# Mixture-of-experts tail of a transformer layer: 39 expert tiles of 128 rows become 25 full tiles and nine tiles of four 32-row units on column groups

## The reference, cut to what matters

```
logits = einsum('btd,ed->bte', x, router_w);  expert = argmax(softmax(logits))
h      = square(relu(einsum('btd,edh->ebth', x, expert_fc)))     # 256 -> 1024, expert_fc 8 x 256 x 1024
out    = einsum('ebth,edh->ebtd', h, expert_proj)                # 1024 -> 256
y      = layernorm(x + out of the token's own expert)
```

## Time and profile before

| | |
|---|---|
| median of 3 runs | 866.6 us (861.0 to 872.18) |
| the profiled execution | 864.4 us, of which the span from first to last instruction 862.6 us |
| mean granted TensorE clock | 0.989 |
| busy share of TensorE / VectorE / ScalarE / GpSimd | 94 / 68 / 32 / 35% |
| DMA | 110.62 MB, 128 GB/s over the span |

### The profile page before, as it was taken

The page is one execution under the profiler, slowest core; times in us unless marked ns, Lnnn a source line. Parts: engine busy times, 40 slices in busy tenths (PEclk is TensorE's granted clock), DMA queues, the critical chain, the costliest instruction groups (busy, mean ns, idle before and its releaser), DMA issues.

```text
span 862.6 us, 19421 instructions
## 1 busy us (share of the span) xinstructions
PE 810.9 (94%) x6910; PEld 653.6 (76%) x6911; DVE 584.7 (68%) x1359; ACT 273.7 (32%) x550; POOL 302.9 (35%) x425
## 2 busy tenths in 40 slices
PE   7979899999999999999999899899989999999995
PEld 3457677677677677677677677688979999999994
DVE  7988878888888888888888846844334444444442
ACT  2324223434434434434434233422112222222220
POOL 8211432414614614614614734633212222222222
PEclk9999999999999999999999999999999999999998
DMA  8899994101001001000000045836535555555540
GB/s 270 266 314 325 298 308 149 49 2 51 25 2 51 25 2 51 25 2 27 25 3 26 26 165 166 282 113 201 183 123 180 185 172 176 178 184 172 176 153 0
DMA packets 69722, 110.62 MB, mean 128 GB/s; under 512 B 5262, under 2 KB 54288, under 8 KB 69649
## 3 DMA queue, kind: packets, MB, share of 16 engines
q1 hardware_dynamic: 66240, 101.17, 37.7%
q0 software_dynamic: 3408, 8.46, 2.6%
HBM read 66.94 MB, written 43.58 MB: 128 GB/s over the span
## 4 chain that ended last, share of the span: by engine, by line
PE 87%; DVE 6%; issue 2%; ACT 2%; POOL 1%; DMA 1%; POOLq 0%; SPq 0%; DVEq 0%; ACTq 0%
PE bank L877 16%; PE bank L866 16%; PE bank L756 7%; PE bank L768 6%; PE bank L788 6%; PE bank L799 6%; PE bank L566 5%; PE bank L718 5%; PE bank L734 4%; PE bank L682 4%; PE bank L575 2%; PE bank L710 2%; PE bank L604 2%; PE bank L596 1%; DVE cc L1302 1%
## 5 line engine op out<-in xcount | busy, mean ns | idle before, releaser
L866 PEld LDWEIGHTS bank<-xsT,fc 128*128 128x128 f32 x1248 | 148.3, 195 | 5.5 <-issue 3.7
L866 PE MATMUL bank<-xsT,fc 128*128 128x128 f32 x1248 | 149.1, 279 | 3.4 <-DVE hT L1588 3.3
L1162 POOL TENSOR_TENSOR rstd<-vare,minus_half 128x1 f32<-128x1 f32 x96 | 53.9, 564 | 266.6 <-DVE vare L1427 266.3
L1048 ACT ACTIVATE relu<-bank 128x512 f32<-128x512 f32 x78 | 46.1, 597 | 205.5 <-PE bank L866 194.9
L877 PE MATMUL bank<-pj,act 128*128 x416 | 94.5, 380 | 1.3 <-issue 1.1
L1418 DVE TENSOR_TENSOR sm<-bank,upto 128x512 f32<-128x512 f32 x128 | 79.4, 684 | 19.7 <-PE bank L682 19.7
L877 PEld LDWEIGHTS bank<-pj,act 128*128 128x128 f32 x416 | 77.0, 190 | 11.6 <-issue 2.2
L1217 POOL TENSOR_TENSOR mrstd<-mvare,minus_half 128x1 f32<-128x1 f32 x39 | 22.1, 567 | 166.0 <-DVE mvare L1606 165.1
L756 PE MATMUL bank<-n1T,w1s 128*128 128x256 f32 x256 | 67.5, 386 | 2.9 <-ACT hT L1000 2.4
L1598 DVE COPY token<-xs 128x1 int32<-128x1 int32 x39 | 6.0, 154 | 93.1 <-PE bank L877 91.6
L788 PE MATMUL bank<-n1T,w1s 128*128 128x256 f32 x256 | 66.8, 383 | 1.3 <-ACT hT L1017 0.8
(11 more groups left out here) (236 smaller groups left out, 1457.5 us busy)
## 6 DMA issues: line engine op xcount, KB each, us to landing
fc<-in_fc SPq DMA_DIRECT2D x39, 1024.0 KB, 5.1
routed_rows<-empty SPq DMA_DIRECT2D x64, 520.0 KB, 9.3
pj<-in_pj SPq DMA_DIRECT2D x8, 1024.0 KB, 11.8
xs<-routed_rows SPq DMA_DIRECT2D x39, 130.0 KB, 2.0
x<-in_x SPq DMA_DIRECT2D x8, 512.0 KB, 3.8
xT<-in_xT SPq DMA_DIRECT2D x7, 512.0 KB, 5.0
w1s<-in_w SPq DMA_DIRECT2D x1, 1024.0 KB, 7.0
w2s<-in_w SPq DMA_DIRECT2D x1, 1024.0 KB, 9.0
```

Source lines behind the costliest of these rows:

```text
L866: last = nc.tensor.matmul(h_bank[n][:, chunk(f)], fc[:, s, k, chunk(4 * n + f)], xsT[:, k, :], start=(k == 0), stop=(k == KT - 1))
L1048: nc.scalar.activation(relu[:, n], src[:], ACT.Relu).then_inc(M["relu"].sem, 1)
L1162: nc.gpsimd.tensor_tensor(rstd[:, n, c], vare[:, n, c], minus_half[:], ALU.pow)\
```

## The change

Each expert now gives only whole tiles of 128 rows to the 25 **full** tiles (`FULL`), and what is left of all experts is cut into **units** of 32 rows. Four units, each of an expert of its own, make a **mixed** tile; there are nine (36 units), at the places 11, 14, 17, 20, 23, 26, 29, 31 and 33 of 34. In a mixed tile:

- the rows of each unit are loaded with a transfer of their own (four of 32 rows), and each unit's up weights with one of 1 MB, into a ring of six buffers (`up_units`, `load_unit_up`);
- `up_mixed` has the rows as the stationary side and the weights as the moving one: 16 calls with 32 stationary and 512 moving columns, the four units on four groups of 32 columns of the array. The hidden values come out not transposed, so `turn_hidden` turns them (8 transposes) and ScalarE copies them (`take_hidden`);
- `down_mixed` has 32 calls with 32 stationary and 256 moving columns on the same groups, with the down weights of each unit in `down_units`, which ScalarE and GpSimd copy there from `pj` ahead of time (`take_down`, two each).

Full tiles from 9 on share two `fc` buffers; the third is in the ring. `units_left` (`d_units`) is a new chain of 22 steps on VectorE after the finish of tile 4, which says what the units are. In VectorE's written order the square of tile 8 now stands ahead of the finish of tile 7. The loops of tiles 9 on are written out, and `down` reads its expert's number right ahead of its first matmul. Cut to its core:

```diff
-SLOTS = NT + E - 1
+FULL = -(-(TOK - E * (P - 1)) // P)                                   # 25
+MIXED = -(-((TOK - FULL * P + E * (UNIT - 1)) // UNIT) // UPT)        # 9
+MIXED_TILES = (11, 14, 17, 20, 23, 26, 29, 31, 33)
+RING = 6
+UP_BUFFER = [n % 3 if n < EARLY else (n - EARLY) % 2 for n in range(FULL)]
...
-    ("m_finish", 4, 0), ("m_square", 6, 0), ("m_finish", 5, 0), ("m_square", 7, 0), ("m_finish", 6, 0),
-    ("m_finish", 7, 0), ("m_square", 8, 0),
+    ("m_finish", 4, 0), ("d_units", 7, 0), ("m_square", 6, 0), ("m_finish", 5, 0), ("m_square", 7, 0), ("m_finish", 6, 0),
+    ("m_square", 8, 0), ("m_finish", 7, 0),
...
+            def load_unit_up(n):
+                e = of_tile(unit_expert, n, E - 1)
+                if n >= RING:
+                    M["up"].wait(sp, MIXED_TILES[(n - RING) // UPT], 2)
+                elif n == RING - 1:
+                    M["up"].wait(sp, EARLY - 1, 2)
+                sp.dma_start(up_units[n % RING][:], fc_d[bass.ds(e, 1)].rearrange("e (k p) n -> p (e k) n", p=P))\
+                    .then_inc(units_in[n // UPT % 2], 16)
...
+            load_rows(EARLY)
+            sp.wait_ge(rt, R_UNITS)
+            for n in range(RING - 1):
+                load_unit_up(n)
+            load_rows(EARLY + 1)
+            load_unit_up(RING - 1)
+            load_rows(EARLY + 2)
+            for j in range(EARLY, SLOTS):
+
+                if of_units(j):
+                    for n in range(UPT * mixed_of(j) + RING, min(UPT * mixed_of(j) + RING + UPT, UNITS)):
+                        load_unit_up(n)
+                elif next_of_buffer(full_of(j)) is not None:
+                    load_up(next_of_buffer(full_of(j)))
+                if EARLY + 3 <= j + 2 < SLOTS:
+                    load_rows(j + 2)
...
+            def up_mixed(j):
+                i = mixed_of(j)
+                M["xsT"].wait(pe, j, 1)
+                pe.wait_ge(units_in[i % 2], 16 * UPT * (i // 2 + 1))
+                for n in range(2):
+                    free_hidden(j, n)
+                    for k in range(KT):
+                        for u in range(UPT):
+                            last = nc.tensor.matmul(h_bank[n][unit(u), :], xsT[:, k, unit(u)],
+                                                    up_units[(UPT * i + u) % RING][:, k, n * 512:n * 512 + 512],
+                                                    start=(k == 0), stop=(k == KT - 1), skip_group_check=True)
+                    last.then_inc(M["up"].sem, 1)
...
+            turn_rows(EARLY)
+            for j in range(EARLY, SLOTS):
+                (up_mixed if of_units(j) else up)(j)
+                if j + 1 < SLOTS:
+                    turn_rows(j + 1)
+                if of_units(j - 1):
+                    down_mixed(j - 1, o_bank)
+                else:
+                    down(j - 1)
+                if of_units(j):
+                    turn_hidden(j)
+            down_mixed(SLOTS - 1, pm)
...
+            def take_down(i, u):
+                if i > 0:
+                    M["down"].wait(pool, MIXED_TILES[i - 1], 1)
+                own = pool.value_load(unit_expert[0:1, UPT * i + u:UPT * i + u + 1], min_val=0, max_val=E - 1)
+                nc.gpsimd.tensor_copy(down_units[u][:], pj[:, bass.ds(own, 1)].rearrange("p a f n -> p (a f) n"))\
+                    .then_inc(own_first, 1)
```

More of the change, by code:

```diff
@@ L385, in build @@
         cleared = sem("cleared")
-        experts_in = [sem(f"expert{e}_in") for e in range(E)]
+        experts_in = sem("experts_in")
+        own_first, own_last = sem("own_first"), sem("own_last")
+        units_in = [sem("up_units_in0"), sem("up_units_in1")]
         fc_in = [sem(f"fc_in{n}") for n in range(3)]
@@ L481, in of_tile, with load_up @@
                 return sp.value_load(at, min_val=0, max_val=most)
[L483 to L494, removed]
+            def load_up(n):
+                e = of_tile(expert, n, E - 1)
+                if n >= 3:
+                    M["up"].wait(sp, max(FULL_TILES[m] for m in range(n) if UP_BUFFER[m] == UP_BUFFER[n]), 2)
+                sp.dma_start(fc[:, UP_BUFFER[n]], fc_d[bass.ds(e, 1)].rearrange("e (k p) n -> p (e k) n", p=P))\
+                    .then_inc(fc_in[UP_BUFFER[n]], 16)
@@ L502, in _ @@
                 sp.wait_ge(scattered[half], 16 * NC * groups)
[L503 to L507, removed]
+            for j in range(3):
+                load_rows(j)
+                load_up(j)
             ev["wo"].wait(sp, G - 1, NC)
@@ new lines, in turn_hidden, with down @@
+            def turn_hidden(j):
+                if mixed_of(j) > 0:
+                    M["act"].wait(pe, MIXED_TILES[mixed_of(j) - 1], 2)
+                for n in range(2):
+                    M["square"].wait(pe, mixed_of(j), n + 1)
+                    for f in range(4):
+                        last = nc.tensor.transpose(again[n][:, chunk(f)], relu[:, n, chunk(f)], ident[:])
+                    last.then_inc(M["again"].sem, 1)
+            def down(j, to=o_bank):
+                own = pe.value_load(expert[0:1, full_of(j):full_of(j) + 1], min_val=0, max_val=E - 1)
+                M["act"].wait(pe, j, 2)
+                M["res"].wait(pe, j - 1, 1)
+                for f in range(FE):
+                    rows = pj[:, bass.ds(own, 1), f, :].rearrange("p a n -> p (a n)")
+                    last = nc.tensor.matmul(to[:, 0:D], actT[j % 3][:, f, :], rows,
+                                            start=(f == 0), stop=(f == FE - 1))
+                last.then_inc(M["down"].sem, 1)
@@ L875, in down @@
                 for f in range(FE):
-                    rows = pj[:, bass.ds(own, 1), f, :].rearrange("p a n -> p (a n)")
-                    last = nc.tensor.matmul(to[:, 0:D], actT[s][:, f, :], rows,
-                                            start=(f == 0), stop=(f == FE - 1))
+                    for u in range(UPT):
+                        last = nc.tensor.matmul(to[unit(u), 0:D], actT[j % 3][:, f, unit(u)], down_units[u][:, f, :],
+                                                start=(f == 0), stop=(f == FE - 1), skip_group_check=True)
                 last.then_inc(M["down"].sem, 1)
@@ L1229, in _ @@
                               "m_store": early_store})
-            with pool.Fori(EARLY // 3, SLOTS // 3) as t:
-                for s in range(3):
-                    store(t, s)
+            pool.wait_ge(rt, R_UNITS)
+            for j in range(EARLY - 1, SLOTS):
+                if j >= EARLY:
+                    store(j)
+                if j == EARLY - 1 or of_units(j) and j < SLOTS - 1:
+                    i = 0 if j < EARLY else mixed_of(j) + 1
+                    for u in range(UPT // 2):
+                        take_down(i, u)
         @block.vector
```

281 lines of the change are left out of this document (171 added, 110 removed).

## The result

| | before | after |
|---|---|---|
| median of 4 runs | 867.8 us (861.0 to 872.2) | 923.8 us (919.2 to 928.0) |
| the profiled execution, and its span | 864.4, 862.6 us | 928.0, 926.0 us |
| mean granted TensorE clock | 0.989 | 0.948 |
| busy share of TensorE | 94% | 88% |

The account below looks back on a forecast made before the run. TensorE, 94% busy, was taken as the bound. Work -29.2, early tiles -5.0 + 2.9, waits behind units +45.7, four-part rows +9, clock +10, reads and steps +6 made 904 us profiled, 906 median; range 884 to 928.

Parts of the forecast that it names:

- TensorE's work, -29.2: All tiles on TensorE: five fewer tiles, mixed ones at 8.03 us against 7.25, cut its work by 29.2 us.
- C: Rival for mixed tiles: narrow calls with long moving sides cost the upper end, units' last piece late; 933 us, chance 8%.
- D: Rival for mixed tiles: column groups don't overlap with 256 and 512 columns; over 1050 us, chance 2%.
- Swap -5.0: Early tiles: squaring tile 8 before finishing tile 7 removes a wait and slow clock at tile 9's up, -5.0 us.
- `d_units` +2.9: Early tiles: 22 VectorE steps after tile 4's y delay up(7) by 2.0 us, plus 0.9 for a possible slow stretch.
- Wait at tile 10, 7.2: Start: tile 10's rows land behind the first five unit loads, so TensorE waits 7.2 us.
- Waits of 5.5: Turns two tiles after a mixed tile: rows behind four unit loads, seven waits of 5.5 us each.
- The waits for rows in four parts: Turns of mixed tiles: their rows, issued as four loads, come 1.1 us late each period, some +9 us in all.
- The clock, +10: After the waits: TensorE's clock falls to its lower level, 1.2 us lost per wait, +10 us in all.
- Reads and steps, +6: Register reads right ahead of the downs, steps between wide and narrow calls, and the end: +6 us.
- Rival B: Waits behind unit loads are half as long, by quicker units or slow clock inside the waits; 875 us, chance 8%.
- Rival A: Rows overtake the unit weights, landing within 3.3 us of issue, so no such waits; 850 us, chance 14%.

Follow-up runs that it names:

- e4: The changed kernel with only its first six unit loads, so later mixed tiles multiply with whatever weights the buffers hold: 862.2 us, ratio 0.996.
- e10: The changed kernel with a fourth rows buffer, spread weight loads, expert's number read ahead of the up, units table made in two parts: 833.5 us, ratio 0.964.
- e1: The kernel before with one line moved, so VectorE squares tile 8 ahead of the finish of tile 7: 861.5 us against 866.4, ratio 0.993.
- e9: The changed kernel with a fourth buffer of rows and rows loads issued a tile earlier, unit loads still bunched: 852.0 us, ratio 0.985.
- e3: The changed kernel with the rows of tiles 12 to 33 issued by GpSimd on its own queue: 973.1 us, ratio 1.123.
- e2: The changed kernel with the rows of the tile after next issued ahead of the four unit loads: 933.8 us, ratio 1.077.
- e12: e10 without its 30 later unit loads, so mixed tiles from the second on use whatever weights the buffers hold: 838.1 us, ratio 0.966.

## Why the prediction was right, and where it wasn't

The forecast, slower by the wait for rows behind four unit loads, came true: 923.8 us for 906, inside its own range (884 to 928), but in its upper part; the profiled execution took 928.0 for 904. e4 puts 61.6 us on those loads, and the waits stand at the turns of tiles 10, 13, 16 and so on, as said.

- **TensorE's work, -29.2: right.** From row to row the mixed up takes 3.57 us and the mixed down 3.59 (forecast 3.46 each, and 0.09 for a step of mode); column groups with 256 and 512 moving columns run at once, so C and D are out. The spans of e10 and of the kernel before differ by 30.0 us, where -29.2, the swap's -5.0, some +3.2 for nine times four steps of mode and +0.7 for ScalarE's last copies make -30.3; a period of 23.09 is 0.2 more than 2 x 7.25 + 8.03 and four steps of mode.
- **Swap -5.0, `d_units` +2.9: right**, the first by e1; of the second 1.7 us were seen, with no slow stretch here (e9 has one behind it, from 612.5 to 615.9).
- **Copies of down weights, nothing: right.** One took 1.91 us on ScalarE (forecast 2.3) and 1.90 on GpSimd (at most 4.9).
- **Wait at tile 10, 7.2: 7.7.** From the same early up (560.45 before, 566.78 after) to the end of tile 11's up the forecast had 197.1 us, and it took 198.0. The 6.3 us ahead of that lie in the groups, whose work is the same; the clock is the likely cause (23.9 us at 0.50 ahead of that up, 3.4 in the kernel before; e9, with 6.8, has 0.75 us of the 6.3).
- **Waits of 5.5: mis-sized.** The seven are 5.8 to 7.6 us, 46.0 for 38.5 in all. The rows landed 14.4 us after the first mixed up and 15.5 after the third (turn at 746.72, mixed up done at 731.21), for 13.9. The microsecond more of the later ones is there at the second of the four units (7.2 us to landing behind tile 11, 8.3 behind tile 17); why wasn't tried.
- **The waits for rows in four parts: mis-sized the other way**, 4.0 for some 9 us; behind a long wait nothing stood ahead of them.
- **The clock, +10: the term that was most wrong.** I took 1.2 us for each wait from a single stretch of 3.40. Behind waits of 6 to 8 us the stretches are 6.83 or 10.24 long, and the turn and the down after each took 1.5 to 3.0 us more than at full clock, 2.3 in the mean of eight: about 9 us more.
- **Reads and steps, +6:** about 4 too little; from a turn to a full down that follows a mixed tile are 0.85 us (689.38 to 690.23), for 0.42.

With the 6.3, these make 22 of the 24 us between 904 and the profiled 928.0. The misses mostly added up, and only the rows in four parts took something back: the range held the time because it left room for longer waits and more slow clock, not because errors cancelled.

**Rival B** (waits half as long) is out too: they were longer. **Rival A** (rows pass the weights, 850) needed them landed 3.3 us after issue; they took 9.3. The Trainium skill says that completion isn't first in, first out per issuing engine (DMA: Bandwidth & Descriptors, Queues, rings and completion order). The traces bear that out by a little only. In the change whole rows behind four unit loads took 9.1 to 10.5 us and landed 0.3 to 0.4 us after the last of them. In e9 the first part of 661.81 landed at 669.3, 1.5 us ahead of the unit issued before it (659.02, landed at 670.8), but the fourth part came 0.7 us after it, and a turn needs all four. On GpSimd's queue (e3) one rows load of six came 1.6 us ahead of the last unit, the others with it.

What the prediction had right was the wait, but not all of its root. It took the order of the queue for the cause, and so the first cure, e2, only moved the wait. The root is the 3 us that three buffers leave a rows load, 0.4 us more than it needed even before. e2 and e9 show it together: in both the rows of the tile after next go ahead of the four units and other rows stand behind them. Without the fourth buffer the waits stay (59.9 us), with it they are gone (7.0), though most landings are longer.

## What to carry to other kernels

Before adding transfers to a queue, take for each transfer already on it the time from the event that frees its buffer to the instruction that needs it, less its landing; here that was 0.4 us, and none of the three orders tried made it enough for the new loads. A buffer more, with the load issued a tile earlier, gave 72 us, where reordering gave 40 at best and another engine's queue lost 49. Read a median of landings by what was in flight at each issue: one number over both kinds hid that the other queue was no way past the weights. Price a wait of TensorE with the slow clock behind it: 6 us of waiting cost 8 here.

## What wasn't expected of the hardware

- The clock's slow stretches behind waits of 6 to 8 us lasted 6.83 or 10.24 us; behind the one wait of 3.3 us of the kernel before it was 3.40.
- Four 1 MB loads held rows behind them on the same queue by 7 us and more (9.1 to 10.5 us, alone 2.0). Rows on another queue, issued while such loads were in flight, mostly landed with the last of them too (3.6 to 5.5 us, with none in flight 2.3 to 2.4; e3).
- 285 GB/s of transfers beside matmuls at full clock cost TensorE nothing that could be measured: 189.50 us for the same work at 285 and at 110 GB/s (e10 and e12).
- GpSimd's issue of a small load took 1.15 us from one to the next (727.61 to 728.76), SyncE's about 0.5 (four in 1.85).
